# The state's transposes amid the convolution's sum, and the experts' weights stored behind the fourth iteration's transfers

## Chip, core and metric

The kernel runs on one core of one Trainium2 chip. The metric is the time of one execution on the device in microseconds, as the median of several runs.

## The reference

16 graphs of 512 nodes with 128 features pass through a graph layer, and all 8192 nodes then pass through a mixture of experts. Cut to what matters:

```python
x = x + gnn(layernorm(x), adj)        # per graph
x = x + ffn(layernorm(x))             # per node

def gnn(x, adj):
    h  = relu(bn1(conv1d(x.T, w1)))                    # 1 tap
    h  = bn2(conv1d(h, w2, pad=8))                     # 17 taps over the nodes
    x_conv = relu(h + x.T).T
    s = x @ w_se.T + b_se                              # 3 numbers per node
    A = exp(-squared_distances(s)) * adj
    x_nmp = A @ relu(x @ w_msg.T + b_msg)
    return gru_cell([x_conv, x_nmp], x)                # gates r, z, n

def ffn(x):                                            # layernorm with gamma, beta inside
    xn = layernorm(x) * gamma + beta
    w = softmax(top_2(xn @ Wr + br))                   # 8 experts, 2 taken
    return sum over e of w[e] * (gelu(xn @ W1[e] + b1[e]) @ W2[e] + b2[e])
```

## The kernel before

The five engines run one hand-ordered instruction stream each, tied by semaphores. All of them walk through `iteration(g, ...)` for g = 0 to 15. Iteration g does the graph layer of graph g up to its new state x1T (feature by node, computed by VectorE at the end of the iteration, L1546), and beside it the router of graph d = g - 1, whose state was finished at the end of iteration g - 1. "Iteration 3" is g = 3, the fourth one. From g = 5 on (`FIRST`) each iteration also runs four tiles of 256 routed rows through the experts (`tile_a`, `tile_b`, `moe`); the other tiles and two graphs done densely follow behind iteration 15, in the tail. GpSimd scatters the rows to the experts' regions in HBM (L1059) and adds the weighed results to the output with indirect DMAs (L1024, in the tail L1045).

Fp32 products are made of three fp32r products (`product`, L571 to L573: high times high, high times low, low times high). The 17-tap convolution is split into three half-size ones: a sum over 9 taps (`conv_sum`, 27 products of 256 columns into PSUM bank C2) and the two differences (`conv_diff`).

The order on TensorE at the head of iteration g is: a tile's first layer (from g = 5), `conv_sum(0, TAPS_A)`, `states(STATES)` for graph d, the second layer of the tile (`tile_b(0)`), the transposes of the messages (L577, into M), `conv_diff(0, 4)`, the distances. `states` (L584) turns x1T by four fp32 products with a widened identity into banks G0 and G2; each is two passes in the trace. It waits for x1T and for `s_f32`, since G2 was read by ScalarE. `conv_sum` bumps `pe_conv_s` when its last tap is done, `states` bumps `pe_outT`.

ScalarE's order beside it is: s and its square, high parts, the tile's gelu, msg, `xlT` (L929), the copies of the turned states (L878, two, which wait for `pe_outT`), then `both` (L937, written to the front of tz, which waits for `pe_conv_s`), then the turned messages (L940) and the exponentials. TensorE's `conv_diff` waits for `both_f32`, since it overwrites the sum in C2. VectorE takes the statistics of the states behind its operands for the distances, multiplies the exponentials by adj, then takes the statistics of the next but one graph's x_ln (L1144), splits xlT of the next graph (L1199), splits xc, and does the router's choice, which ends with the running counts `pre` (L1233). TensorE's counting product (L770) waits for these.

SyncE issues the loads and stores of an iteration in this order: [g = 3 only: the store of w_s to w_all, L492], the tile loads from g = 5 on, the store of the new states (L502, waits for the copies), x_ln for g + 2 (L505), adj for g + 1 (L508), x_res for g (L512), and at the end of iterations 4 to 14 the first two tile loads of the next iteration. w_s holds the prepared weights of all 8 experts (3136 KB); the tiles' weights are loaded from w_all. Its three waits (`w12_ready`, `w2_loaded`, `b1_set`) are for the parts of w_s, the last of which VectorE writes at the head of iteration 3. At the end of iteration 4 SyncE waits for `w12_stored` before the first tile load.

Of the kernel before, what the change touches and what calls it, by code (L numbers as in the profile page):

```python
# [7 lines left out]
F32 = mybir.dt.float32  # L8
# [59 lines left out]
TAPS_A = (TAPS + 1) // 2  # L68
# [96 lines left out]
def gnn_moe(nc, x, x_t, adj_t, weights, vectors, consts, pads, routed, w_all, out):  # L165
# [4 lines left out]
    with ExitStack() as ctx:  # L170
# [9 lines left out]
        with ExitStack() as early:  # L180
            def once(name, shape, dt=F32):
                return early.enter_context(nc.sbuf_tensor(name, shape, dt))
# [4 lines left out]
            w_s = once("w_s", [P, EXPERTS, XCOLS], F32R)  # L187
# [139 lines left out]
        w1_loaded, w2_loaded, w1_hi, w12_ready, w12_stored = map(  # L327
            sem, ("w1_loaded", "w2_loaded", "w1_hi", "w12_ready", "w12_stored"))
        beta_set, pe_br, br_set, pe_b1, b1_set = map(sem, ("beta_set", "pe_br", "br_set", "pe_b1", "b1_set"))
# [49 lines left out]
        def tile_of(g, j):  # L379

            n = SLOTS * (g - FIRST) + j
            return n, n % RING, 16 * (n // RING + 1)

        def x1_of(d):
            return x1s[d % 2] if d < ROUTED else x1_d[d - ROUTED]
# [52 lines left out]
        def _(sp):  # L438
# [22 lines left out]
            def tile_loads(j, at, e):  # L461
                sp.dma_start(xt[j][:], routed[bass.ds(at, TILE), :].rearrange("(t p) c -> p t c", p=P)).then_inc(
                    xt_in[j], 16)
                sp.dma_start(w_t[j][:].bitcast(F32), w_all[bass.ds(e, 1), :, :].rearrange("e p h -> p (e h)")).then_inc(
                    w_in[j], 16)

            def choice(table, i):
                at = sp.value_load(t_start[table][0:1, i:i + 1], min_val=0, max_val=DUMMY + (LAST - 1) * TILE)
                e = sp.value_load(t_expert[table][0:1, i:i + 1], min_val=0, max_val=EXPERTS - 1)
                return at, e  # L470
# [8 lines left out]
            def iteration(g, tail, more, moe):  # L479
                d = g - 1  # L480

                def batch_load(of, j):
                    n, slot, loads = tile_of(of, j)
                    if n >= RING:
                        sp.wait_ge(added, 16 * TT * (n - RING + 1))
                    tile_loads(slot, *chosen[j])

                if g == 3:
                    sp.wait_ge(w12_ready, 2)
                    sp.wait_ge(w2_loaded, 16)  # L490
                    sp.wait_ge(b1_set, 1)
                    sp.dma_start(w_all.rearrange("e p h -> p e h"), w_s[:].bitcast(F32)).then_inc(w12_stored, 16)  # L492

                if moe:
                    sp.wait_ge(x1T_ready, d + 1)
                    batch_load(g, 2)
                if tail:
                    sp.wait_ge(x1_ready, d + 1)
                    if moe:
                        batch_load(g, 3)  # L500
                    if d < ROUTED:
                        sp.dma_start(out_v[d], x1_of(d)[:, :, 0:P]).then_inc(out_set[d % 2], 16)  # L502
                if g < GRAPHS - 2:
                    sp.wait_ge(xl_ready, g + 2)
                    sp.dma_start(x_ln[:], x_v[g + 2]).then_inc(x_ln_loaded, 16)  # L505
                if more:
                    sp.wait_ge(a_prod, NT * g + NT)
                    sp.dma_start(adj[:], adj_v[g + 1]).then_inc(adj_loaded, 16)  # L508
                if FIRST - 1 <= g < GRAPHS - 1:

                    sp.wait_ge(tab_step, TAB_STEPS * (g - 1 - TAB_FIRST))
                sp.dma_start(x_res[:], x_t[g]).then_inc(x_res_loaded, 16)  # L512
                if g == FIRST - 1:
                    sp.wait_ge(w12_stored, 16)
                    sp.wait_ge(pads_stored, 64)
                if FIRST - 1 <= g < GRAPHS - 1:
                    chosen[:] = [choice(g % 2, j) for j in range(SLOTS)]
                    for i in range(2):
                        sp.wait_ge(rows_out[i], 16 * NT * TOP * ((g - i) // 2))
                    for j in range(2):  # L520
                        batch_load(g + 1, j)
                if g == 1:
                    sp.dma_start(routed[DUMMY + TAKEN:, :], pads[TAKEN:, :]).then_inc(pads_stored, 16)
                if g == 2:
                    sp.dma_start(out[TOKENS + TAKEN:, :], pads[TAKEN:, 0:P]).then_inc(pads_stored, 16)

            chosen = []
            run(iteration)


# [36 lines left out]
        def _(pe):  # L567
            ident = cst[:, C_ID:C_ID + P]

            def product(psum, w, rhs_h, rhs_l, start=True, stop=True):  # L570
                pe.matmul(psum, hi(w), rhs_h, start=start, stop=False)  # L571
                pe.matmul(psum, hi(w), rhs_l, start=False, stop=False)  # L572
                return pe.matmul(psum, lo(w), rhs_h, start=False, stop=stop)  # L573
# [6 lines left out]
            def states(banks):  # L580

                for t in range(NT):
                    at = t % 2 * STATE
                    last = pe.matmul(banks[t // 2][:, at:at + STATE], x1T[:, t * P:(t + 1) * P], ident_wr[:], start=True,  # L584
                                     stop=True)
                last.then_inc(pe_outT, 1)
# [6 lines left out]
            def conv_sum(a, b):  # L593
                for i in range(a, b):
                    w = CONV_S + i if i < TAPS_B else CONV_A + i
                    last = product(C2[:, 0:HALF], w, cv_h[:, 2, i:i + HALF], cv_l[:, 2, i:i + HALF],
                                   start=(i == 0), stop=(i == TAPS_A - 1))
                if b == TAPS_A:
                    last.then_inc(pe_conv_s, 1)
# [42 lines left out]
            def second(m, w):  # L642

                rows_of = YO[bank_set(m)][:, 0:TILE]
                pe.wait_ge(gelu_done, m + 1)
                if m > 0:
                    pe.wait_ge(y_done, m if m <= STREAMED else m - 1)
                pe.matmul(rows_of, w[:, X_SEL:X_SEL + 1].broadcast_to([P, P]), b2_r[:, :, :].rearrange("p t d -> p (t d)"),  # L648
                          start=True, stop=False)
                for t in range(TT):  # L650
                    for h in range(HALVES):
                        last = pe.matmul(rows_of[:, t * P:(t + 1) * P], ge[m % 2][:, h, t * P:(t + 1) * P],  # L652
                                         w[:, X_W2 + h * P:X_W2 + (h + 1) * P].bitcast(F32), start=False,
                                         stop=(t == TT - 1 and h == HALVES - 1))
                last.then_inc(pe_y, 1)
# [15 lines left out]
            def iteration(g, tail, more, moe):  # L671
# [8 lines left out]
                def tile_b(j):  # L680
                    if moe:
                        second(tile_of(g, j)[0], w_t[tile_of(g, j)[1]])
# [7 lines left out]
                def bias_products(first):  # L690

                    if is_graph(g, 1) or is_graph(g, 2):
                        for n in range(first + 2 * (g - 1), first + 2 * g):
                            last = pe.matmul(H0[:, n:n + 1], w1_raw[:, n * P:(n + 1) * P], vec[:, V_BETA:V_BETA + 1],
                                             start=True, stop=True)
                        last.then_inc(pe_b1, 1)
# [6 lines left out]
                pe.wait_ge(odd_split, g + 1)  # L703
                if tail:
                    pe.wait_ge(gate_step, 2 * d + 2)
                conv_sum(0, TAPS_A)
                if tail:
                    pe.wait_ge(x1T_ready, d + 1)
                    pe.wait_ge(s_f32, g + 1)
                    states(STATES)  # L710
                tile_b(0)
                bias_products(4)
                pe.wait_ge(msg_f32, g + 1)
# [92 lines left out]
            head(0)  # L806
            idle(IDLE_CONV)
            run(iteration)

            g = GRAPHS - 1  # L810
# [887 lines left out]
```

## Time and profile before

| | us |
|---|---|
| median of 3 runs | 612.37 (612.35 to 612.53) |
| the profiled execution | 611.76 |
| its span | 610.0 |
| TensorE busy | 584.5 (96%) |
| VectorE busy | 477.9 (78%) |
| ScalarE busy | 369.5 (61%) |
| GpSimd busy | 336.6 (55%) |

The granted TensorE clock was full almost throughout. Busy times are sums over one execution. A matmul's recorded time overlaps that of the next one, so what counts on TensorE is the distance from start to start, and the idle time in front of an instruction. In the rows below PE is TensorE, PEld its weight loads, DVE VectorE, ACT ScalarE, POOL GpSimd, SP SyncE. Times are microseconds from the start of the span.

### The profile page before, as it was taken

Reading aid. Unit: us, or ns where it says so; the run is one execution under the profiler, and the core shown is the slowest. Engines: PE = TensorE matmul, PEld = TensorE weight load, DVE = VectorE, ACT = ScalarE, POOL = GpSimd, SP = SyncE. Lnnn points to the kernel's source line nnn. Section 1 sums busy time; section 2 is a strip of 40 time slices with the busy share of each in tenths; the row PEclk is TensorE's granted clock in tenths of the full one; section 3 lists DMA queues with packets and bytes.
Section 4 is the critical chain, followed back from the end, with each engine's and each line's share of the span. In section 5 each row is a group of like instructions: output and inputs, shape, how many; then the busy total and the mean of one; then the engine's idle time right before and its main releaser. Section 6 shows DMA issues by size and latency. Waiting matters only on the chain. (4 is left out here: it accounts for less than half of the span.)

```text
span 610.0 us, 12899 instructions
## 1 busy us (share of the span) xinstructions
PE 584.5 (96%) x3936; PEld 515.1 (84%) x3936; DVE 477.9 (78%) x2014; ACT 369.5 (61%) x733; POOL 336.6 (55%) x249
## 2 busy tenths in 40 slices
PE   8999999899999999999999999999999999999990
PEld 6877878587879797979898989898898979999990
DVE  7989889698888888888989797979788966644330
ACT  5664636365857584848485857667675745655550
POOL 2000504133367776767677776768576663555775
PEclk9999999999999999999999999999999999999996
DMA  8515376325466657575655665757556777766863
GB/s 299 202 71 198 117 232 254 123 73 183 121 186 145 195 134 202 132 201 139 172 154 152 153 172 144 197 135 191 145 149 152 219 162 204 157 153 153 223 102 43
DMA packets 85860, 99.72 MB, mean 163 GB/s; under 512 B 7520, under 2 KB 62560, under 8 KB 85472
## 3 DMA queue, kind: packets, MB, share of 16 engines
q1 hardware_dynamic: 64064, 82.37, 43.4%
q0 software_dynamic: 21728, 16.53, 16.5%
q8 instruction: 32, 0.52, 0.3%
q14 instruction: 36, 0.29, 0.1%
HBM read 74.95 MB, written 30.39 MB: 173 GB/s over the span
## 5 line engine op out<-in xcount | busy, mean ns | idle before, releaser
L1024 POOL DMA_INDIRECT out<-y_t,xt x88 | 158.6, 1802 | 89.6 <-DMA out<-y_t,xt 55.6
L1059 POOL DMA_INDIRECT routed<-row,at_u x112 | 115.7, 1033 | 140.8 <-DVE at_u L1268 108.5
L571 PE MATMUL C<-cv_h,w_hi 128*128 128x256 f32 (+1 forms) x432 | 127.9, 296 | 2.9 <-ACT tz L937 1.4
L573 PE MATMUL C<-cv_h,w_lo 128*128 128x256 f32 (+1 forms) x432 | 123.3, 286 | 0.0
L572 PE MATMUL C<-cv_l,w_hi 128*128 128x256 f32 (+1 forms) x432 | 123.2, 285 | 0.0
L571 PEld LDWEIGHTS C<-cv_h,w_hi 128*128 128x128 f32 x432 | 81.6, 189 | 6.1 <-ACT tz L937 3.2
L572 PEld LDWEIGHTS C<-cv_l,w_hi 128*128 128x128 f32 x432 | 81.5, 189 | 0.9
L573 PEld LDWEIGHTS C<-cv_h,w_lo 128*128 128x128 f32 x432 | 81.4, 188 | 0.7
L761 PE MATMUL G<-ex,msg_t 128*128 128x512 f32 x128 | 57.7, 593 | 0.0
L652 PE MATMUL Y<-w_t,ge 128*128 128x128 f32 x424 | 55.8, 274 | 0.0
L652 PEld LDWEIGHTS Y<-w_t,ge 128*128 128x128 f32 x424 | 51.7, 191 | 3.1 <-issue 2.6
L857 ACT ACTIVATE ge<-H,w_t 128x256 f32<-128x256 f32 x106 | 44.4, 471 | 7.7 <-PE H L624 7.2
L1350 DVE TENSOR_TENSOR xT_l<-H,xT_h 128x256 fp32r<-128x256 f32 x53 | 22.1, 417 | 31.8 <-ACT xT_h L850 31.8
L761 PEld LDWEIGHTS G<-ex,msg_t 128*128 128x128 f32 x128 | 23.1, 190 | 23.0 <-issue 23.0
L1483 DVE TENSOR_TENSOR ex<-ex,adj 128x512 f32<-128x512 f32 x64 | 39.7, 678 | 0.0
L571 PE MATMUL G<-xlT_h,w_hi 128*128 128x512 f32 x96 | 38.2, 398 | 0.6 <-DVE xlT_l L1199 0.6
L573 PE MATMUL G<-xlT_h,w_lo 128*128 128x512 f32 x96 | 38.0, 395 | 0.0
L572 PE MATMUL G<-xlT_l,w_hi 128*128 128x512 f32 x96 | 37.8, 393 | 0.0
L969 ACT ACTIVATE tr<-G,dv 128x512 f32<-128x512 f32 x16 | 11.0, 688 | 42.8 <-PE G L573 42.8
L1045 POOL DMA_INDIRECT out<-adj,ids x16 | 24.9, 1555 | 21.3 <-issue 16.2
L622 PE MATMUL H<-xT_h,w_t 128*128 128x256 f32 x106 | 32.1, 302 | 0.1
L965 ACT CAST cv_h<-G 128x512 fp32r<-128x512 f32 x16 | 9.4, 586 | 36.4 <-PE G L761 36.4
(273 smaller groups left out, 1616.3 us busy)
## 6 DMA issues: line engine op xcount, KB each, us to landing
w_t<-w_all SPq DMA_DIRECT2D x63, 392.0 KB, 3.7
adj<-adj_t SPq DMA_DIRECT2D x16, 1024.0 KB, 5.8
xt<-routed SPq DMA_DIRECT2D x63, 144.0 KB, 3.1
wd<-w_all SPq DMA_DIRECT2D x11, 392.0 KB, 4.9
x_ln<-x SPq DMA_DIRECT2D x16, 256.0 KB, 2.9
x_res<-x_t SPq DMA_DIRECT2D x16, 256.0 KB, 6.1
out<-x SPq DMA_DIRECT2D x15, 256.0 KB, 4.1
w_all<-w_s SPq DMA_DIRECT2D x1, 3136.0 KB, 10.6
```

Source lines behind the costliest of these rows:

```text
L571: pe.matmul(psum, hi(w), rhs_h, start=start, stop=False)
L572: pe.matmul(psum, hi(w), rhs_l, start=False, stop=False)
L573: return pe.matmul(psum, lo(w), rhs_h, start=False, stop=stop)
L622: pe.matmul(half, w[:, h * P:(h + 1) * P], x_h, start=True, stop=False)
L652: last = pe.matmul(rows_of[:, t * P:(t + 1) * P], ge[m % 2][:, h, t * P:(t + 1) * P], w[:, X_W2 + h * P:X_W2 + (h + 1) * P].bitcast(F32), ...
L761: last = pe.matmul(G0[:], msg_t[:, j, :], ex[:, j, :], start=(j == 0), stop=(j == NT - 1))
L857: last = nc.scalar.activation(ge[m % 2][:, h, :], HID[bank_set(m)][:, h * TILE:(h + 1) * TILE], ACT.Gelu, bias=w[:, X_B1 + h:X_B1 + h + 1] ...
L1024: nc.gpsimd.indirect_dma_start(out=out, out_offset=bass.IndirectOffsetOnAxis(ap=xt[j][:, t, R_ID:R_ID + 1].bitcast(U32), axis=0), in_=y_t[ ...
L1045: nc.gpsimd.indirect_dma_start(out=out, out_offset=bass.IndirectOffsetOnAxis(ap=ids[:, i, t:t + 1], axis=0), in_=y_last[i][:, t, :], in_of ...
L1059: nc.gpsimd.indirect_dma_start(out=routed, out_offset=bass.IndirectOffsetOnAxis(ap=ats_u[d % 2][:, n:n + 1], axis=0), in_=rows[d % 2][:, n ...
L1350: nc.vector.tensor_tensor(xT_l[n % 2][:], XT[s][:, 0:TILE], xT_h[n % 2][:].bitcast(F32), ALU.subtract).then_inc(xT_split, 1)
L1483: nc.vector.tensor_tensor(ex[:, j, :], ex[:, j, :], adj[:, j, :], ALU.mult).then_inc(a_prod, 1)
```

## The change

Two edits, no other. On TensorE `conv_sum` is called in two parts, taps 0 to 4 and taps 5 to 8, and the states' transposes stand between them with their two waits. They write to other banks (G0, G2) than the open sum (C2). On SyncE the store of w_s in iteration 3, with its three waits, moves from the head of the iteration's transfers to behind the load of x_res.

```diff
-                if g == 3:
-                    sp.wait_ge(w12_ready, 2)
-                    sp.wait_ge(w2_loaded, 16)
-                    sp.wait_ge(b1_set, 1)
-                    sp.dma_start(w_all.rearrange("e p h -> p e h"), w_s[:].bitcast(F32)).then_inc(w12_stored, 16)
-
                 if moe:
                     sp.wait_ge(x1T_ready, d + 1)
                     batch_load(g, 2)
...
                 sp.dma_start(x_res[:], x_t[g]).then_inc(x_res_loaded, 16)
+                if g == 3:
+                    sp.wait_ge(w12_ready, 2)
+                    sp.wait_ge(w2_loaded, 16)
+                    sp.wait_ge(b1_set, 1)
+                    sp.dma_start(w_all.rearrange("e p h -> p e h"), w_s[:].bitcast(F32)).then_inc(w12_stored, 16)
                 if g == FIRST - 1:
                     sp.wait_ge(w12_stored, 16)
                     sp.wait_ge(pads_stored, 64)
...
-                conv_sum(0, TAPS_A)
+                conv_sum(0, 5)
                 if tail:
                     pe.wait_ge(x1T_ready, d + 1)
                     pe.wait_ge(s_f32, g + 1)
                     states(STATES)
+                conv_sum(5, TAPS_A)
                 tile_b(0)
```

## Rows read from the trace of the kernel before

**Rows 1.** The page, part 1: engine, busy time, share, instructions.

```profile
PE 584.5 (96%) x3936; PEld 515.1 (84%) x3936; DVE 477.9 (78%) x2014; ACT 369.5 (61%) x733; POOL 336.6 (55%) x249
```

**Rows 2.** Waits: who waited for what, total us, times, longest.

```profile
DVE st L1144 <- DMA x_ln<-x: 3.1, 1, 3.1
```

**Rows 3.** Order of time, SyncE, iteration 3: start, us, line, what.

```profile
96.66 0.38 SPq L492 DMA_DIRECT2D w_all<-w_s  x1
...
104.18 0.38 SPq L505 DMA_DIRECT2D x_ln<-x  x1
...
107.00 0.63 SPq L512 DMA_DIRECT2D x_res<-x_t  x1
```

**Rows 4.** The page, part 6: DMA issues, KB each, median us to landing.

```profile
w_all<-w_s SPq DMA_DIRECT2D x1, 3136.0 KB, 10.6
```

**Rows 5.** Order of time, VectorE, iteration 3; in brackets the idle time before.

```profile
111.14 0.87 DVE L1144 BATCH_NORM_STATS2 st<-x_ln 128x6 f32<-128x128 f32 x4 [3.12 <-DMA x_ln<-x]
...
116.11 0.77 DVE L1233 TENSOR_TENSOR pre<-pre,sel 128x8 fp32r<-128x8 f32 x4
...
122.17 0.69 DVE L1536 SCALAR_TENSOR_TENSOR gr<-gr,x_res 128x512 f32<-128x512 f32 x1
```

**Rows 6.** Order of time, TensorE, iteration 3: messages' product and counting product.

```profile
109.08 3.60 PE L761 MATMUL G<-ex,msg_t 128*128 128x512 f32 x8
...
116.94 0.27 PE L770 MATMUL C<-pre,ones_r 128*128 128x8 f32 x1 [1.40 <-DVE pre L1233]
```

**Rows 7.** Order of time, TensorE, iteration 4: the same two.

```profile
137.81 3.60 PE L761 MATMUL G<-ex,msg_t 128*128 128x512 f32 x8
...
143.06 0.27 PE L770 MATMUL C<-pre,ones_r 128*128 128x8 f32 x1 [0.24 <-DVE pre L1233]
```

**Rows 8.** Order of time, iteration 2: states, copies, next convolution product, VectorE's split.

```profile
70.15 1.09 PE L584 MATMUL G<-ident_wr,x1T 128*128 128x136 f32 x8
...
71.28 0.67 ACT L878 COPY x<-G 128x272 f32<-128x272 f32 x2 [0.25 <-PE G L584]
...
72.47 0.39 PE L571 MATMUL C<-cv_h,w_hi 128*128 128x256 f32 x1 [0.40 <-ACT tz L937]
...
83.77 0.69 DVE L1199 TENSOR_TENSOR xlT_l<-M,xlT_h 128x512 fp32r<-128x512 f32 x1 [1.39 <-ACT xlT_h L888]
```

**Rows 9.** Order of time, head of iteration 3: VectorE, TensorE, ScalarE.

```profile
95.09 0.69 DVE L1546 SCALAR_TENSOR_TENSOR x1T<-tz,gr 128x512 f32<-128x512 f32 x1
...
96.97 1.09 PE L584 MATMUL G<-ident_wr,x1T 128*128 128x136 f32 x8
...
97.75 0.58 ACT L929 COPY xlT<-M 128x512 f32<-128x512 f32 x1
98.22 0.69 ACT L878 COPY x<-G 128x272 f32<-128x272 f32 x2
...
99.42 0.39 PE L571 MATMUL C<-cv_h,w_hi 128*128 128x256 f32 x1 [0.32 <-ACT tz L937]
```

**Rows 10.** Order of time, iteration 7: VectorE, TensorE's weight loads, ScalarE.

```profile
214.42 0.69 DVE L1546 SCALAR_TENSOR_TENSOR x1T<-tz,gr 128x512 f32<-128x512 f32 x1
...
217.93 0.19 PEld L573 LDWEIGHTS C<-cv_h,w_lo 128*128 128x128 f32 x1
218.05 1.00 PEld L584 LDWEIGHTS G<-ident_wr,x1T 128*128 128x128 f32 x8
...
219.85 0.58 ACT L937 ACTIVATE tz<-C,dv 128x256 f32<-128x256 f32 x1
...
219.99 0.47 PEld L577 LDWEIGHTS M<-cst,ex 128*128 128x128 f32 x4
220.48 0.19 PEld L571 LDWEIGHTS C<-cv_h,w_hi 128*128 128x128 f32 x1
```

**Rows 11.** Order of time, start of the tail: VectorE's weighing, GpSimd's first add.

```profile
514.03 0.42 DVE L1371 TENSOR_TENSOR adj<-Y,own_w 128x256 f32<-128x256 f32 x1
...
515.80 1.55 POOL L1045 DMA_INDIRECT out<-adj,ids  x1 [4.75 <-DMA out<-y_t,xt]
```

## The prediction

> **What bounds the kernel now.** I read the parts of the page first, then the waits, then the order of time around the two places that the change touches. TensorE (PE) is busy 96% of the span [rows 1], so a microsecond is won only where PE's stream has a hole, or where something later than PE paces the end. The waits view has few long entries on VectorE (DVE) in the first iterations, but one stands out: 3.1 us, once, for the landing of x_ln [rows 2]. The time-ordered rows say where: in iteration 3 SyncE (SP) issues the store of the experts' weights at 96.66, the load of x_ln at 104.18, the one of x_res at 107.00 [rows 3]. The store needs 10.6 us to land [rows 4]. So the store holds the DMA engines until 107.2, and DVE starts its statistics only at 111.14 after 3.12 us of idle; without the wait it would have started at 108.02 [rows 5]. DVE runs in order, so the router's last sums (pre) end at 116.88 [rows 5], and PE, which starts the messages' product at 109.08, reaches the counting product only at 116.94, held by DVE [rows 6].
>
> **Part 1, the store moved behind x_res.** It removes no instruction and adds none: one DMA issue (0.38 us of SP) and its three waits go past the out store, x_ln, adj and x_res on SP. Its waits are then long met. Behind it on SP stands only the out store of iteration 4, which waits for that iteration's states anyway, so no issue is held up. What it is worth is read from iteration 4, which has the same stages without a late load: from the start of the messages' product (137.81) to the counting product (143.06) there are 5.25 us [rows 7]; in iteration 3 there are 116.94 - 109.08 = 7.86 [rows 6]. The difference is 2.61 us. Not all 3.12 us of DVE's idle comes back, because DVE then waits for the next thing: xlT_h, which follows PE's own transposes just ahead of the messages' product. Iteration 2 shows that wait, 1.39 us [rows 8]; in iteration 3 it comes to about 3.12 - 2.61 = 0.5. That is what is late next, and it is in the 2.61 already. Bounds: 0 (the wait is met by something else) and 3.12; I take **2.6**, the row of the twin iteration.
>
> The store's own 10.6 us now run from about 112 (adj and x_res, issued ahead, go first) to about 123. Nothing waits for it until the first tile loads at the end of iteration 4. An iteration is 28.7 us long here (109.08 to 137.81) [rows 6, 7], and the loads belong to the end of the next one, so over 10 us of cover are left; if it were gone, each microsecond would be paid by SP and then by PE at iteration 5.
>
> **Part 2, the state's transposes behind the fifth tap.** Removed: nothing. Moved: eight passes (four fp32 products), and the two waits ahead of them (x1T, s_f32), ahead of twelve of the sum's 27 products. PE's work is the same. The one dearer product after a change from fp32 to fp32r occurs once in either order: before, it is the bias product of the tile behind the states, after, it is the first product of tap six, and the tile's bias then follows an fp32r product. So 0 on PE itself. What the move changes is what ScalarE (ACT) finds: it copies the states, and only then evicts the sum (tz), for which PE's next products wait.
>
> The sum's products are issued 0.12 us apart (217.93 to 218.05) [rows 10], so the states move forward by twelve times 0.12, 1.44 us, unless x1T is later. Three kinds of iteration:
>
> Iteration 2: ACT idles 0.25 us ahead of the state copies, waiting for them, and PE idles 0.40 ahead of the next convolution product, waiting for tz [rows 8]. With the states early the copies start right behind xlT; there the next instruction starts 0.11 us ahead of the recorded end of the one before (97.75 + 0.58 = 98.33 against 98.22) [rows 9]. So the copies and tz come 0.25 + 0.11 = 0.36 earlier, within the 0.40 that PE idles. It is kept, since DVE waits for PE's transposes in this iteration (the 1.39 above), not PE for DVE. **0.36**, bounds 0 and 0.36. The sum itself ends 0.96 later than now (eight passes and the dearer product), but its end plus 0.3 still lies ahead of the copies' end.
>
> Iterations 1, 3, 4 and 5: nothing. In iteration 3 the copies follow xlT with no idle time, tz follows them, and PE starts at 99.42 behind tz [rows 9]; ACT's chain isn't touched. Here the moved wait is visible: x1T ends at 95.09 + 0.69 = 95.78, while tap five would be through at 96.97 - 1.44 = 95.53 [rows 9]. PE stalls some 0.25 us there, in iteration 4 the same. Queued behind it are taps six to nine; the sum then ends near 98.4, and ACT reaches tz only near 98.8 (PE's 99.42 less tz's 0.58 [rows 10]). Price 0 as long as ACT's copies are later; if that cover were gone, 2 x 0.25 = 0.5. In iteration 1 PE waits for DVE's split of the differences, in 5 for ACT's late gelu.
>
> Iterations 6 to 15 (one stands for ten, all alike): x1T ends at 214.42 + 0.69 = 215.11, tap five at 218.05 - 1.44 = 216.61, so 1.5 us to spare [rows 10]. The next convolution's weight load waits for tz, which ends at 219.85 + 0.58 = 220.43. Four loads of the transposes ahead take 0.11 each from 219.99, so it could start at 220.43; it starts at 220.48 [rows 10]. With tz a few tenths earlier, as in iteration 2, that 0.05 goes, ten times: **0.5**, bounds 0 and 0.6.
>
> The waits inside the sum: at the old place the first states' load starts 0.12 us behind the last of the sum [rows 10], the spacing of the sum's own products, with both waits standing between. Waits that are met cost PE nothing. The Trainium skill (Advanced Engine Details and Errata, section Network/Comms) puts a sequencer's reading of a semaphore at 50 to 100 ns. By that rule two waits in fifteen iterations would be 1.5 to 3.0 us if the new place made them bare; by the row it is 0, and the row decides.
>
> **Does it reach the end?** Behind iteration 15 the tail is paced by GpSimd's (POOL's) adds: its first one starts at 515.80, 1.35 us after DVE has weighed that tile (514.03 + 0.42 = 514.45), having waited for a landing [rows 11]. POOL's adds wait for landings that share the DMA engines with SP's loads, and those are paced by PE, so POOL should move with PE. Two things pull apart: the states' earlier copies let SP issue the fourth tile's loads about 0.4 us sooner (the 0.36 of iteration 2) (a gain for landings, at most 0.4 at the last hand-over), and POOL may not follow the ten steps of 0.05 (a loss, at most 0.5). I take 0.
>
> **Sum.** 2.6 + 0.36 + 0.5 = 3.5 us. The profiled execution took 611.76 us (span 610.0); 611.76 - 3.5 = 608.3. It lies 0.61 below the median of 612.37, so the forecast for the median is 612.37 - 3.5 = **608.9**.
>
> **Rivals.**
> A, the forecast: 608.9, with its own range 608.4 to 609.4. Chance 0.52.
> B, only the store counts: the 0.36 and the 0.05s are given back at PE's next wait or by POOL. 612.37 - 2.6 = 609.8. For it: POOL already runs behind at the tail [rows 11]. Chance 0.18.
> C, the tail gives more: loads and copies sooner by 0.4 in the last iterations shorten a landing that POOL waits for, 0.4 to 1.0 us. 608.2. Chance 0.12.
> D, the POOL-paced tail keeps part of the gain: POOL's adds in iterations 14 and 15 wait for landings that don't move; 1.0 to 2.0 us are left. 610.4 to 611.4. Against it: the gain arises in iteration 3, four hundred microseconds ahead. Chance 0.07.
> E, the two waits inside the sum cost each iteration the spacing of one product, 15 x 0.12 = 1.8 us: 610.7. Against it is the spacing at the old place [rows 10]. Chance 0.04.
> F, the change doesn't do what it says: the late x_ln has another cause than the store (the out store or a slow landing), and only part 2 acts: 612.37 - 0.9 = 611.5. Against it: the store's landing at 96.66 + 10.6 = 107.2 and x_ln's being used at 111.14 fit a line in which the transfers follow one another. Chance 0.04.
> G, slower: the store shares the DMA engines with adj and x_res rather than following them. DVE reads x_res at 122.17 [rows 5], 119.5 after the change. In flight from 107 on are adj (128 x 2048 numbers, 1.0 MB), x_res (128 x 512, 0.25) and the store's 3.1 MB; at the store's pace (3136 KB in 10.6 us, 0.30 MB/us) [rows 4] they land by 121.5, which costs 2 us and leaves 610.9. From a landing later than 123 it is slower than before; at 0.25 MB/us (POOL's scatters of graph 2 run at the same time) it is 124.4, 4.9 us late: 612.37 - 3.5 + 4.9 = 613.8. Against it: x_ln, issued behind the store, came after it and not with it. Chance 0.03.
>
> **How the numbers follow.** A, B and C hold 0.82 of the chance; their bounds give 607.8 to 610.3. A measurement of this kernel can tell about 0.2% (1.2 us) from no change. Faster by more than that: A, B, C, and most of D and E, 0.90. Within it: F, and the low ends of D and E, 0.07. Slower: G, 0.03.
>
> **What would show it right or wrong.** In the new profile: SP issues w_all behind x_res near 107; DVE's wait for x_ln is gone and one of about 0.5 us for xlT_h stands in iteration 3; from the messages' product to the counting product there are 5.25 us in iteration 3, not 7.86; in iteration 2 the copies start with no idle time; in iterations 3 and 4 a hole of 0.25 us stands ahead of the states and no later start of the next convolution product; from iteration 6 on the period between like instructions falls by 0.05. The forecast is wrong if x1T comes after tap five from iteration 6 on, if DVE waits for x_res, or if POOL's first tail add moves by less than PE's last iteration.

## The result and the profile after

The changed kernel takes **609.0 us** (median of five, 607.84 to 609.91) where the kernel before takes 612.37 (five runs, 611.38 to 612.89). The ratio is 0.9945, with a 95% interval of 0.993 to 0.9961. That is 3.4 us, and faster by more than the 0.2% that can be told from no change. The profiled execution took 607.84 us (span 606.0) and is the quickest of the five, 1.2 below their median; the one of before (611.76) lies 0.6 below its own. So the two traces differ by 3.9 us, and the medians by 3.4.

The changed kernel's code stands one line higher up to the moved call: its products are L570 to L572 (before L571 to L573), its states L583. First the page, part 1, to be held against [rows 1]. TensorE's busy time has fallen by 0.8, its share is the same.

```profile
PE 583.7 (96%) x3936; PEld 514.6 (85%) x3936; DVE 478.9 (79%) x2014; ACT 368.4 (61%) x733; POOL 333.4 (55%) x249
```

**The store.** SyncE's issues of iteration 3 in order of time (start, length of the issue, line, transfer), to be held against [rows 3]:

```profile
98.62 0.38 SPq L496 DMA_DIRECT2D out<-x  x1
103.86 0.37 SPq L499 DMA_DIRECT2D x_ln<-x  x1
106.27 0.37 SPq L502 DMA_DIRECT2D adj<-adj_t  x1
106.68 0.51 SPq L506 DMA_DIRECT2D x_res<-x_t  x1
107.31 0.38 SPq L511 DMA_DIRECT2D w_all<-w_s  x1
124.72 0.38 SPq L496 DMA_DIRECT2D out<-x  x1
```

The store (w_all) is issued last, and no other issue is late for it. VectorE in the same stretch (in brackets the idle time ahead, and what ended it), beside [rows 5]:

```profile
107.63 0.86 DVE L1144 BATCH_NORM_STATS2 st<-x_ln 128x6 f32<-128x128 f32 x4
109.56 0.69 DVE L1199 TENSOR_TENSOR xlT_l<-M,xlT_h 128x512 fp32r<-128x512 f32 x1 [0.44 <-ACT xlT_h L888]
113.14 0.77 DVE L1233 TENSOR_TENSOR pre<-pre,sel 128x8 fp32r<-128x8 f32 x4
```

The 3.12 us of idle time ahead of the statistics are gone, and a new wait of 0.44 for xlT_h stands behind them. On TensorE the messages' product and the counting product, beside [rows 6]:

```profile
108.74 3.60 PE L761 MATMUL G<-ex,msg_t 128*128 128x512 f32 x8
113.96 0.27 PE L770 MATMUL C<-pre,ones_r 128*128 128x8 f32 x1 [0.23 <-DVE pre L1233]
```

113.96 - 108.74 = 5.22 us, where before had 7.86.

**The states.** Iteration 2 on ScalarE and TensorE, beside [rows 8]: the copies of the states (L878) start right behind xlT, and the next convolution product at 72.16 instead of 72.47.

```profile
68.76 1.09 PE L583 MATMUL G<-ident_wr,x1T 128*128 128x136 f32 x8
70.48 0.58 ACT L929 COPY xlT<-M 128x512 f32<-128x512 f32 x1
70.95 0.69 ACT L878 COPY x<-G 128x272 f32<-128x272 f32 x2
72.16 0.39 PE L570 MATMUL C<-cv_h,w_hi 128*128 128x256 f32 x1
```

Iteration 7, beside [rows 10]: the states follow tap five at the products' own spacing of 0.12 us (213.66 to 213.78), and the convolution's weight load stands directly behind the load ahead of it.

```profile
213.66 0.28 PE L572 MATMUL C<-cv_h,w_lo 128*128 128x256 f32 x1
213.78 1.09 PE L583 MATMUL G<-ident_wr,x1T 128*128 128x136 f32 x8
...
216.44 0.63 ACT L937 ACTIVATE tz<-C,dv 128x256 f32<-128x256 f32 x1
217.03 0.47 PEld L576 LDWEIGHTS M<-cst,ex 128*128 128x128 f32 x4
217.14 0.60 PE L576 MATMUL M<-cst,ex 128*128 128x128 f32 x4
217.47 0.19 PEld L570 LDWEIGHTS C<-cv_h,w_hi 128*128 128x128 f32 x1
217.50 0.36 PE L570 MATMUL C<-cv_h,w_hi 128*128 128x256 f32 x1
```

The same product starts at 185.60 one iteration earlier: the period is 217.50 - 185.60 = 31.90 us, against 31.93 before.

**The end.** GpSimd's first add of the tail, beside [rows 11], and its last:

```profile
512.26 1.55 POOL L1045 DMA_INDIRECT out<-adj,ids  x1 [6.95 <-DVE adj L1371]
...
599.27 1.55 POOL L1045 DMA_INDIRECT out<-gh,ids  x1 [0.30 <-issue]
```

The first add comes 515.80 - 512.26 = 3.5 us earlier than before, and no longer waits for a landing. The last one started at 603.22 before, 3.95 us later.

### The profile page after: what moved, and what is told of

Read it like the earlier page. It is cut to its first block and busy times, and to the rows that moved or that the text cites. A ratio compares the mean times of both kernels' runs of the same rounds, so it can differ in the third digit from the quotient of the medians.

```text
span 606.0 us, 12899 instructions
## 1 busy us (share of the span) xinstructions
PE 583.7 (96%) x3936; PEld 514.6 (85%) x3936; DVE 478.9 (79%) x2014; ACT 368.4 (61%) x733; POOL 333.4 (55%) x249
## 5 line engine op out<-in xcount | busy, mean ns | idle before, releaser
L1024 POOL DMA_INDIRECT out<-y_t,xt x88 | 155.5, 1767 | 90.0 <-DMA out<-y_t,xt 52.3
L570 PE MATMUL C<-cv_h,w_hi 128*128 128x256 f32 (+1 forms) x432 | 129.1, 299 | 2.6 <-ACT tz L937 1.0
L571 PE MATMUL C<-cv_l,w_hi 128*128 128x256 f32 (+1 forms) x432 | 123.4, 286 | 0.0
L572 PE MATMUL C<-cv_h,w_lo 128*128 128x256 f32 (+1 forms) x432 | 123.3, 285 | 0.0
L570 PEld LDWEIGHTS C<-cv_h,w_hi 128*128 128x128 f32 x432 | 81.7, 189 | 5.5 <-ACT tz L937 2.9
L571 PEld LDWEIGHTS C<-cv_l,w_hi 128*128 128x128 f32 x432 | 81.5, 189 | 0.9
L572 PEld LDWEIGHTS C<-cv_h,w_lo 128*128 128x128 f32 x432 | 81.5, 189 | 0.7
L570 PE MATMUL G<-xlT_h,w_hi 128*128 128x512 f32 x96 | 38.2, 398 | 0.6 <-DVE xlT_l L1199 0.6
L572 PE MATMUL G<-xlT_h,w_lo 128*128 128x512 f32 x96 | 37.9, 395 | 0.0
L571 PE MATMUL G<-xlT_l,w_hi 128*128 128x512 f32 x96 | 37.8, 393 | 0.0
```

Of the source, the lines that this page charges most:

```text
L1024: nc.gpsimd.indirect_dma_start(out=out, out_offset=bass.IndirectOffsetOnAxis(ap=xt[j][:, t, R_ID:R_ID + 1].bitcast(U32), axis=0), in_=y_t[ ...
```

## The experiments

Seven edited kernels ran in four sessions, each beside runs of the kernel before; four of them and the changed kernel ran a second time, which makes twelve runs. Two kinds of session showed up, and the difference matters. In the first and the last, the kernel before took 612.6 and 612.9 us, near the 612.4 above. In the second and the third it took 622.2 and 622.7. A ratio is therefore always against the kernel before of the same session.

### The parts alone, and the place in the sum

**e1_store_only**: the kernel before, with the store alone moved.

```diff
-                if g == 3:
-                    sp.wait_ge(w12_ready, 2)
-                    sp.wait_ge(w2_loaded, 16)
-                    sp.wait_ge(b1_set, 1)
-                    sp.dma_start(w_all.rearrange("e p h -> p e h"), w_s[:].bitcast(F32)).then_inc(w12_stored, 16)
...
                 sp.dma_start(x_res[:], x_t[g]).then_inc(x_res_loaded, 16)
+                if g == 3:
+                    sp.wait_ge(w12_ready, 2)
+                    sp.wait_ge(w2_loaded, 16)
+                    sp.wait_ge(b1_set, 1)
+                    sp.dma_start(w_all.rearrange("e p h -> p e h"), w_s[:].bitcast(F32)).then_inc(w12_stored, 16)
```

> Only the store of w_s moves behind x_res; the states' transposes stay behind the whole sum. My theory (the two parts add: 2.6 us from the store, 0.3 from iteration 2, 0.3 from the ten later iterations): 609.7 us, 2.6 below before and about 0.7 above the changed kernel; from the messages' product to the counting product in iteration 3 there are 5.25 us, in iteration 2 the 0.40 us hole ahead of the next convolution product is back, and the period from iteration 6 on is 31.93 us, not 31.90. Rival (the store does all of it, and what the states gain is lost in the tail): 609.0, the same as the changed kernel.

Measured: 609.74 us beside 612.64, ratio 0.9955 (0.994 to 0.9969), 2.9 us. TensorE's two products of iteration 3 are 5.22 us apart, as in the changed kernel, and the period later on is the old one. The page, part 6, has the store's landing (KB, median us):

```profile
w_all<-w_s SPq DMA_DIRECT2D x1, 3136.0 KB, 14.9
```

At its new place it takes 14.9 us instead of 10.6 [rows 4], from 107.65 to 122.5. No instruction waits for it there.

**e2_states_only**: the kernel before, with the states alone moved.

```diff
-                conv_sum(0, TAPS_A)
+                conv_sum(0, 5)
...
                     states(STATES)
+                conv_sum(5, TAPS_A)
```

> Only the states' transposes move behind tap five; the store stays at the head of iteration 3. My theory: VectorE still waits 3.1 us for x_ln, PE is 0.3 us earlier after iteration 2 and 0.6 to 0.7 earlier by iteration 15, so 611.7 us against 612.37 before. Rival (SyncE's earlier loads in the last iterations shorten landings that GpSimd waits for): 610.5 to 611.2. Rival (nothing reaches the end): 612.4.

Measured: 612.03 us, ratio 0.9995 (0.9981 to 1.0009): 0.6 us less by the medians, and an interval that holds no change too. The sum of the parts, 2.9 + 0.6 = 3.5, is close to the 3.4 of the whole change. The trace holds a surprise. The gain of iteration 2 is there (the counting product comes at 87.77 instead of 88.17), and in iteration 3 it comes at 116.45 instead of 116.94, but in iteration 4 at 143.87, 0.81 us behind the kernel before (143.06). TensorE by stretch (width, busy time and instructions, granted clock, DMA share, GB/s):

```profile
100.00:112.00 12.00, 12.00 (x70) 1.00 1.00 344
112.00:118.00 6.00, 3.38 (x14) 1.00 0.02 9
118.00:122.00 4.00, 4.00 (x13) 0.57 0.10 37
```

and the products behind the hole in order of time:

```profile
118.08 0.40 PE L572 MATMUL G<-cv_l,w_hi 128*128 128x512 f32 x1
118.32 0.59 PE L573 MATMUL G<-cv_h,w_lo 128*128 128x512 f32 x1
118.71 0.63 PE L571 MATMUL G<-xlT_h,w_hi 128*128 128x512 f32 x1
```

TensorE idled 2.6 us of six, in two pauses of 1.12 and 1.40 us and a few tenths, while VectorE was held by x_ln, and then the granted clock was 0.57 in a stretch of four: most of it ran at the lower of its two levels, 1.2 GHz instead of 2.4, and a product of 512 columns took 0.63 instead of 0.40 us. The kernel before idles as long in the same six (2.7 us) and kept its clock in its profiled execution:

```profile
112.00:116.00 4.00, 2.34 (x8) 1.00 0.06 24
116.00:118.00 2.00, 0.97 (x5) 1.00 0.00 0
118.00:120.00 2.00, 2.00 (x11) 1.00 0.00 0
120.00:122.00 2.00, 2.00 (x10) 1.00 0.10 37
```

From 0.49 ahead to 0.81 behind makes 1.3 us for the clock. So the late landing has a second price, which falls in some executions and not in others. The mean clock of each execution fits that: in the sessions near 612 us it is 0.989 or less in 20 of 51 executions with the store at the head (the kernel before and e2), and in 1 of 40 with the store behind x_res. In e2 the seven with the lower clock have a median of 612.85 us and the other five 610.96; in the kernel before beside them it is 613.03 (nine) against 611.75 (nineteen). These executions have no trace, so that their clock fell in the same place isn't shown.

**e3_tap_two**: the changed kernel, with the states behind tap two instead of five.

```diff
-                conv_sum(0, 5)
+                conv_sum(0, 2)
...
                     states(STATES)
-                conv_sum(5, TAPS_A)
+                conv_sum(2, TAPS_A)
```

> The changed kernel with the states behind tap two instead of tap five. My theory of the cover: in iterations 2 to 4 x1T then comes 1.0 to 1.3 us after the last product ahead of the states, the seven taps behind them end later than ScalarE reaches tz, and PE's next convolution product starts 0.7 to 0.8 us later in each of the three; iterations 1 and 5 are held by something else, and from 6 on x1T is still in time. Sum 2.2 us: 611.2, against 609.0 for tap five. Rival (PE's stall at the states is always made up, since VectorE and ScalarE pace these iterations): 609.0. Rival (every microsecond of stall is paid): 609.0 + 3.5 + 0.25 = 612.8.

Measured: 611.12 us, ratio 0.998 (0.9968 to 0.9992), 1.5 us faster than before and some 2 slower than the changed kernel. Iteration 3 on both engines:

```profile
96.34 1.19 PE L583 MATMUL G<-ident_wr,x1T 128*128 128x136 f32 x8 [1.22 <-DVE x1T L1546]
100.69 0.39 PE L570 MATMUL C<-cv_h,w_hi 128*128 128x256 f32 x1 [0.22 <-ACT tz L937]
...
98.72 0.69 ACT L878 COPY x<-G 128x272 f32<-128x272 f32 x2
100.07 0.56 ACT L937 ACTIVATE tz<-C,dv 128x256 f32<-128x256 f32 x1 [0.66 <-PE C L572]
```

TensorE now stalls 1.22 us for x1T, with seven taps queued behind. The sum ends so late that ScalarE waits 0.66 us for it before tz, and the next product is late. From the first product of the sum it takes 0.75 to 0.8 us longer to get there in iterations 2, 3 and 4 than in the changed kernel, 2.3 in all. The cover that the prediction named (ScalarE's copies are later than the sum) is there, and it ends.

**e4_sum_first**: the changed kernel, with the sum whole ahead of the states, and ScalarE's tz ahead of the copies of the states (the last four edited lines are ScalarE's; between them stands the eviction of the sum to tz).

```diff
-                conv_sum(0, 5)
+                conv_sum(0, TAPS_A)
...
                     states(STATES)
-                conv_sum(5, TAPS_A)
...
-                if tail:
-                    states(d, STATES)
...
+                if tail:
+                    states(d, STATES)
```

> The store behind x_res as in the changed kernel, the states behind the whole sum as before, and on ScalarE the eviction of the sum (tz) ahead of the two copies of the states. If the states' copies ahead of tz are what PE's next convolution product waits for, this frees more than moving the transposes: PE starts that product 0.25 us earlier than in the changed kernel in iteration 2 and about 0.5 earlier in 3, 4 and 5. Kept where VectorE has room (it waits 0.3 to 1.3 us for PE in iterations 2 and 3), lost in iteration 4, where it has none: 1.0 to 1.3 us, 607.8 us. Rival (VectorE paces iterations 2 to 5, and it gets the states later): 609.0 or above.

Measured: 607.96 us, ratio 0.992 (0.9903 to 0.9937). It was run again in the last session:

> The kernel with the sum whole ahead of the states and its eviction (tz) ahead of their copies, once more, to see whether its lead holds on another chip. On a chip like the first (a kernel before near 612.5): 607.9 again, ratio 0.992. On a chip where TensorE's signals arrive late in iterations 2 to 4 (a kernel before near 622.5), the store's place is worth nothing, since the late x_ln is covered there; what is left is the order of tz and the copies, worth 4.7 - 2.9 = 1.8 us: ratio 0.997. Rival: the order is also worth nothing there, because tz and the copies then wait for the same late signal: ratio 0.998 to 1.

Measured there: 607.91 beside 612.88, ratio 0.9919 (0.9905 to 0.9933). It beats both kernels, the changed one by 1.0 to 1.1 us by the medians, though the intervals of the ratios just meet (at 0.993), and the two were never run in one session. ScalarE in iteration 3, and the next convolution product:

```profile
97.27 0.58 ACT L928 COPY xlT<-M 128x512 f32<-128x512 f32 x1
97.73 0.58 ACT L934 ACTIVATE tz<-C,dv 128x256 f32<-128x256 f32 x1
98.19 0.68 ACT L877 COPY x<-G 128x272 f32<-128x272 f32 x2
...
97.99 0.63 PE L576 MATMUL M<-cst,ex 128*128 128x128 f32 x4 [0.42 <-ACT xlT L928]
98.37 0.38 PE L570 MATMUL C<-cv_h,w_hi 128*128 128x256 f32 x1
```

What TensorE waits for (tz) goes first, what only the router needs goes second, and TensorE has no idle time ahead of the product (the 0.42 us ahead of the transposes is a wait for xlT). By the starts of the next state product (C<-xc_h), iteration 2 takes 26.60 instead of 26.91 us, iteration 3 25.62 instead of 26.11 and iteration 5 31.90 instead of 32.24; iteration 4 gains nothing (26.31 against 26.27), as expected. From iteration 6 on next to nothing is added (a period of 31.89). In iteration 15 that product starts 1.0 us earlier than in the changed kernel (461.37 against 462.37). In the two profiled executions the tail takes it back (last add at 599.68 against 599.27), so the lead to the end rests on the medians.

### Sessions in which the store's place is worth little

Three kernels on the order of transfers went into the second session.

**e5_store_ahead_of_x_res**: the changed kernel with x_res issued behind the store.

```diff
-                sp.dma_start(x_res[:], x_t[g]).then_inc(x_res_loaded, 16)
                 if g == 3:
...
                     sp.dma_start(w_all.rearrange("e p h -> p e h"), w_s[:].bitcast(F32)).then_inc(w12_stored, 16)
+                sp.dma_start(x_res[:], x_t[g]).then_inc(x_res_loaded, 16)
```

> The changed kernel with the store issued ahead of the load of x_res, behind adj. If transfers of SyncE's queue follow one another in the order of issue, x_res lands with the store near 123 us, VectorE needs it near 119.3, and the wait of 3.5 us is paid in full: 612.5. If they share the engines evenly, x_res (256 KB) lands after a few microseconds of its own, long before it is needed: 609.0.

Measured: 620.34 beside 622.18, ratio 0.9975 (0.9962 to 0.9988).

**e6_store_twice**: the kernel before with a second store of the same size behind the first.

```diff
                     sp.dma_start(w_all.rearrange("e p h -> p e h"), w_s[:].bitcast(F32)).then_inc(w12_stored, 16)
+                    sp.dma_start(w_spare.rearrange("e p h -> p e h"), w_s[:].bitcast(F32)).then_inc(w12_stored, 16)
```

> The kernel before with a second store of w_s, to a spare tensor in HBM, right behind the first; it adds 3136 KB of traffic and no other work. If the place of x_ln behind the store is the whole cause of VectorE's 3.1 us wait, the wait grows by the second store's 10 us to about 13.5, and that is paid one for one: 622.7 us. Rival (the late x_ln has another cause, such as the out store): 612.4 to 613.

Measured: 626.72, ratio 1.0065 (1.0043 to 1.0087). 4 us slower by the ratio, not 10. VectorE waits 5.4 us for x_ln. (SyncE's wait ahead of the first tile loads was raised to both stores, here and in the next kernel.)

**e7_store_halves**: the kernel before with one half of the store at the old place and one at the new.

```diff
-                    sp.dma_start(w_all.rearrange("e p h -> p e h"), w_s[:].bitcast(F32)).then_inc(w12_stored, 16)
+                    sp.dma_start(w_all[0:4].rearrange("e p h -> p e h"), w_s[:, 0:4].bitcast(F32)).then_inc(w12_stored, 16)
...
                 sp.dma_start(x_res[:], x_t[g]).then_inc(x_res_loaded, 16)
+                if g == 3:
+                    sp.dma_start(w_all[4:8].rearrange("e p h -> p e h"), w_s[:, 4:8].bitcast(F32)).then_inc(w12_stored, 16)
```

> The kernel before with the store in two halves: four experts at the old place at the head of iteration 3, four behind x_res. The first half lands near 102 us, the out store near 103, both before x_ln is issued at 104.2, so VectorE's wait is gone as with the whole store moved: 612.37 - 2.6 = 609.7. If instead any store at the head costs its share, half of the 2.6 stays: 611.1.

Measured: 622.24, ratio 0.9987 (0.997 to 1.0005), no gain, though VectorE doesn't wait for x_ln. All three missed in the same direction: the store's place was worth less than it should be. So they were repeated in a third session beside the changed kernel itself as a control.

> The changed kernel itself, as the control beside the next three. Two theories of why the store's place was worth less in the last three runs. First: it was the chip. There ScalarE stood 3.5 us ahead of the states' copies in iterations 3 and 4, VectorE came 3.3 us later to x_ln, and most of the late landing was covered. Then on a chip without that idle time this kernel is 3.5 us faster than the kernel before, and on one with it less than 1 us faster. Second: the chip doesn't matter, and the ratio is 0.994 on either.

**e8_changed_again** measured: 621.48 beside 622.69, ratio 0.9986 (0.9964 to 1.0008), 1.2 us. The very kernel that gained 3.4 gains 1.2 here, and the interval holds no change too. That rules out the second theory (0.994 on either). The first is right in that the late signals go with the small gain, but it isn't the chip by its number: the third session and the last both ran on the chip numbered 2, the third with the kernel before at 622.7 and the last at 612.9. Nor is it quite fixed for a session: one of the ten executions of e9, below, took 615.55 us. Its ScalarE and VectorE in iteration 3, and TensorE:

```profile
98.81 0.58 ACT L929 COPY xlT<-M 128x512 f32<-128x512 f32 x1
102.86 0.67 ACT L878 COPY x<-G 128x272 f32<-128x272 f32 x2 [3.48 <-remote]
...
103.57 0.87 DVE L1144 BATCH_NORM_STATS2 st<-x 128x6 f32<-128x128 f32 x4 [3.21 <-ACT x L878]
113.55 0.86 DVE L1144 BATCH_NORM_STATS2 st<-x_ln 128x6 f32<-128x128 f32 x4
...
96.90 1.19 PE L583 MATMUL G<-ident_wr,x1T 128*128 128x136 f32 x8
104.06 0.51 PE L570 MATMUL C<-cv_h,w_hi 128*128 128x256 f32 x1 [3.90 <-ACT tz L937]
```

TensorE's states are recorded as done at 96.90 + 1.19 = 98.09, but ScalarE idles until 102.8 and then copies them. "Remote" means that the profile names no instruction at the moment of the signal. The signals of the states, of the sum and of the messages' transposes, whose records end at 98.09, 99.50 and 100.16, all arrive between 102.8 and 103.1. TensorE idles 3.90 us until tz is written, and then its clock falls: two stretches of TensorE in this kernel and a product at their end,

```profile
91.00:104.00 13.00, 8.98 (x57) 1.00 0.14 48
104.00:108.00 4.00, 3.94 (x16) 0.57 0.23 66
...
108.05 0.28 PE L570 MATMUL C<-cv_h,w_hi 128*128 128x256 f32 x1
```

and the same two products in the changed kernel's first trace:

```profile
99.12 0.39 PE L570 MATMUL C<-cv_h,w_hi 128*128 128x256 f32 x1 [0.32 <-ACT tz L937]
...
101.57 0.28 PE L570 MATMUL C<-cv_h,w_hi 128*128 128x256 f32 x1
```

The same work between them takes 108.05 - 104.06 = 3.99 us instead of 101.57 - 99.12 = 2.45: 1.5 us for the clock. The longer idle time (3.90 against 0.32) and the clock account for the 5.1 us by which iteration 3 is longer (31.21 between the counting products, 26.10 in the first trace). Iteration 4 is longer by 4.7 and iteration 2 by 1.2: 11.0 of the 12.2 us between the spans. From iteration 6 on the period is 31.90 nearly throughout, as without late signals.

This also says why the store matters less. VectorE reaches x_ln at 113.55, and SyncE issues x_ln at 108.40, by which time a store issued at the head has landed (issued at 97.40, landed 10.5 us later in e10, below). So the late signals cover the store. The kernel before has no trace from such a session; what speaks for it is that e7 and e11 (below), which read x_ln without a wait, are no faster than the kernel before beside them.

**The three again** in the third session:

> The whole change with the store one place earlier, between adj and x_res, once more. If VectorE's wait for x_ln is all that the store's place decides, this equals the changed kernel of the same call within 0.5 us wherever x_res lands before VectorE reads it. If the transfers follow one another in the order of issue, x_res lands behind the store near 119.5 and costs up to 1 us, for it is read at 119.5. On a chip without ScalarE's idle time: 609.0 or 610 against a kernel before at 612.4.

**e9** measured 620.94, ratio 0.9964 (0.9938 to 0.999), equal to the control within the intervals. The order of transfers is seen on VectorE:

```profile
127.66 0.69 DVE L1536 SCALAR_TENSOR_TENSOR gr<-gr,x_res 128x512 f32<-128x512 f32 x1 [2.03 <-DMA x_res<-x_t]
```

x_res, issued at 112.47 just behind the store (111.18), arrives some 15 us later, where ahead of the store it took 7.0 (106.68 to 113.63 in the changed kernel). e5, its like, read x_res at 125.89 with no such wait. Those 2.03 us cost nothing here: iteration 4 is as long as in e8 (30.82 us between the counting products in both), and TensorE's next convolution product starts at 134.75 in e9 and 134.85 in e8, in both after a late signal of iteration 4.

> The kernel before with a second store of the same size right behind the first. The first theory (order of the transfers, covered by ScalarE's idle time on the last chip): on a chip without that idle time x_ln lands some 10 us later than in the kernel before, VectorE waits 13 us for it, and the kernel is 10 us slower, near 622.5. On a chip with it: 4 us slower, as the last time. The rival, that the late x_ln has another cause than the store: no slower than the kernel before by more than 1 us.

**e10** measured 625.31, ratio 1.0049 (1.0028 to 1.0069), 2.6 us slower by the medians, 3.0 by the ratio. The first store lands in 10.5 us, the second, issued 0.43 later, in 19.8 (at 117.6), and x_ln behind it:

```profile
119.10 0.87 DVE L1145 BATCH_NORM_STATS2 st<-x_ln 128x6 f32<-128x128 f32 x4 [5.59 <-DMA x_ln<-x]
```

VectorE waits 5.6 us and not 13, since it comes later by itself. So the late x_ln is the store's doing: doubled, it brings the wait back even here. The rival that it has another cause is out.

> The kernel before with half of the store at its old place and half behind x_res. By the order of transfers the first half lands by 102.9, before x_ln is issued at 104, so that it costs nothing: on a chip without ScalarE's idle time 609.8, as with the whole store moved alone. If a store of half the size still delays x_ln by half (1.3 us kept): 611.1. On a chip with that idle time: within 0.5 us of the kernel before, as the last time.

**e11** measured 622.94, ratio 0.9997 (0.9973 to 1.002), like the kernel before, as was expected for such a session. The first half lands in 5.6 us (issued at 98.06), ahead of x_ln's issue (108.88). What the halves are worth beside timely signals wasn't run. As an estimate from that landing they would cost x_ln nothing: issued at 96.7, gone by 102.3, with x_ln issued at 104.2.

## Why the prediction was right, and for which sessions

**The store: right in mechanism and size.** Forecast 2.6 from the twin iteration. The two products stand 5.22 us apart (forecast 5.25), which is 2.64 less than before, and alone the move gave 2.9 us. The 0.5 us that were said to be late next are the 0.44 for xlT_h. What the prediction put at nothing is the clock: it priced the store by TensorE's waits alone, and the executions in which the clock falls behind these waits (1.3 us in e2's trace) are rarer with the store moved. The traced terms add up to 2.64 + 0.31 + 0.33 = 3.3 us. That the forecast sum of 3.5 and the medians' 3.4 lie so close is partly luck, since this term and the tail (below) are in the one and not in the other.

**Iteration 2: right, a little small.** Forecast 0.36, measured 72.47 - 72.16 = 0.31. It reaches the counting product (88.17 to 87.86).

**Iterations 3 and 4: right.** In iteration 3 the states start at 95.53, 0.05 behind the end of x1T and 0.29 behind where tap five would let them, and the next convolution product starts as soon after the sum's first as before (5.68 us, before 5.66). In iteration 4 it is the same (states at 121.64, 0.06 behind x1T; 5.67 us in both kernels). e3 shows the same stall at 1.22 us, where the cover ends.

**Iterations 6 to 15: right mechanism, wrong size.** "With tz a few tenths earlier that 0.05 goes, ten times": the hole did go (the weight load at 217.47 follows the one before directly), but the period fell by 0.033, and ten are 0.33, not 0.5. The other 0.017 us came back between the sum's last product, the tile's bias and its second layer (216.02, 216.13, 216.25), which now follow one another without the states between; the prediction had put 0 for them. In e4, which closes the hole in another way, the period is 31.89.

**Waits that are met cost TensorE nothing: right.** The states' first product starts 0.12 us behind tap five's last, the spacing of the sum itself (213.54, 213.66, 213.78). Rival E (1.8 us) is out. By the rule of the Trainium skill (Advanced Engine Details and Errata, section Network/Comms), 50 to 100 ns for a sequencer's reading of a semaphore, two bare readings would, as an estimate, have shown as 0.1 to 0.2 us more; the trace shows none at this place.

**The tail: not settled.** The prediction took 0. In the profiled execution the last add is 3.95 us earlier while TensorE's state product of iteration 15 is 3.25 earlier (465.61 to 462.37), so the tail gave some 0.7. In the profiled execution of e1 it took 0.3 (2.26 us against 2.59), and in that of e4 0.7 (3.54 against 4.24). One execution each doesn't tell a steady gain from scatter; the medians show 3.4 for all of it.

**Rivals.** B (only the store) would have been 609.8; e1 measured 609.74, and the whole change lies 0.7 below it. By the times alone that isn't clear (the intervals of the two ratios overlap); by the trace it is, since the 0.31 and the 0.33 us are still there at iteration 15. C (608.2, the tail gives more) lies below the five executions' median, but the spread of the tail leaves it open for one execution. D is out by the trace, F by the trace and by e10. Part of G, that adj and x_res lose a little to the store, can be seen: x_res takes 7.0 us to land, and 5.6 in iteration 4 of the kernel before. Its price is out: x_res, issued ahead of the store, landed at 113.63 and VectorE read it without a wait, since the transfers went in the order of issue for the greater part and the store gave way (14.9 us in e1 instead of 10.6). e9 shows the wait, 2.03 us, when that order is turned round.

**What the prediction didn't see** is that its largest term hangs on VectorE being early at x_ln. In two of four sessions VectorE was some 6 us later there, half the store moved gave nothing (e7, e11), and the change gave 1.2 us (interval from 2.2 faster to 0.5 slower). With e5 and e9, the changed kernel but for one place in the order, it is 1.2 to 1.8 us by the medians, two of the three clear of no change. Nothing in the one trace of before could show it, but the question could be asked: by how much may the waiting engine be late before the wait is worth nothing? The answer stood in [rows 5], 3.12 us.

## What to carry to other kernels

Look for a large store that is issued ahead of small loads: here x_ln, issued 7.5 us behind the store, took 6.9 us to land and 3.2 without it. What it's worth to move the store is read from a twin stage without it, not from the idle time of the engine that waits. Where two engines' orders meet (sum, states, copies), first ask which of ScalarE's results TensorE waits for and put that one first: that gave some 1 us more than moving TensorE's own work. And a gain that removes a wait of 3 us is gone wherever the waiting engine comes 3 us later, so measure it in more than one session, and beside the kernel before each time.

## What the runs showed of the hardware

TensorE's signals came late in all seven traces of the second and the third session, and cost time in iterations 2 to 4. In iteration 3, three signals whose products are recorded as ending over 2 us apart arrived within 0.3 us of one another, the first some 4.7 us late; in iteration 4 the same, with the first 3.4 to 4.8 us late, save in e9, where x1T itself came later; in iteration 2 the last of the three was late by up to 2.8 us. In all five traces of the other sessions, and in both of the first comparison, no such signal is late by over 0.3 us. It costs some 10 us of 612 with either order of transfers. What holds them back is open: between 92 and 106 us the traces of e8 and of the changed kernel show the same kinds of transfers (0.86 and 1.02 MB), the chip's number doesn't decide it, and the profile names no releaser.

Idle time of 2.6 us (two pauses, e2) and of 3.9 us (one, e8) in TensorE's work was followed by four microseconds at a granted clock of 0.57, which cost 1.3 and 1.5 us on top of it. Idle time of 2.7 us in the kernel before was not, in its one trace.
